# Second layer norm of six sequences: two ScalarE activations each in place of one VectorE operation

## The reference, cut to what matters

```python
x = x + tanh(g_xattn) * attention(layernorm(x), ctx, ctx, mask, Wq, Wk, Wv, Wo)   # 32 heads, 8 kv heads
x = x + tanh(g_ffn)   * ffn(layernorm(x), 4-bit gate, up and down weights)        # inner width 1376

def layernorm(x): return (x - mean(x)) / sqrt(var(x) + 1e-5)
```

## Time and profile before

| | us |
|---|---|
| median of 3 runs | 774.27 (773.15 to 774.89) |
| the profiled execution | 772.95 |
| its span, first to last instruction | 771.1 |
| granted TensorE clock, mean | 0.983 of full speed |
| `score(59)` to the first product of sequences 4 to 7 (start to start) | 540.70 to 605.39 |

### The profile page before, as it was taken

How to read it: one execution, slowest core, us unless ns; L and a number is a source line. 1 busy time by engine, 2 the same in 40 slices (tenths; PEclk the granted TensorE clock), 3 DMA queues, 4 the chain that set the end, 5 groups by cost and what they waited for, 6 DMA issues and landing times. The chain is left out here.

```text
span 771.1 us, 11053 instructions
## 1 busy us (share of the span) xinstructions
PE 727.8 (94%) x3394; PEld 602.3 (78%) x3394; DVE 602.1 (78%) x924; ACT 430.2 (56%) x777; POOL 509.8 (66%) x386
## 2 busy tenths in 40 slices
PE   3989999999999999999999999999669689999998
PEld 3868888888888888888888888888546578888786
DVE  6688798878879887987888788888877678778521
ACT  4686666665666666566666656565543345555420
POOL 5577778776677877667777766775796376656400
PEclk9999999999999999999999999999999899999999
DMA  9421012001201200120120002003220234432011
GB/s 278 102 80 42 1 42 96 14 1 40 85 1 41 96 15 1 31 93 1 42 95 15 1 28 96 1 0 84 48 65 0 66 89 96 116 97 41 1 69 41
DMA packets 70621, 41.53 MB, mean 54 GB/s; under 512 B 23242, under 2 KB 63050, under 8 KB 70570
## 3 DMA queue, kind: packets, MB, share of 16 engines
q1 hardware_dynamic: 70570, 40.90, 18.6%
HBM read 38.77 MB, written 2.11 MB: 53 GB/s over the span
## 5 line engine op out<-in xcount | busy, mean ns | idle before, releaser
L583 POOL TENSOR_TENSOR aT_lo<-attn,aT_hi 128x512 fp32r<-128x512 f32 x64 | 83.1, 1298 | 94.5 <-ACT aT_hi L802 94.5
L55 PE MATMUL ps_o<-wo_hi,aT_hi 128*128 128x512 f32 x256 | 102.2, 399 | 1.8 <-POOL acc L589 1.6
L55 PE MATMUL bank_q<-xT_hi,wq_hi 128*128 128x512 f32 x256 | 100.2, 391 | 2.4 <-DVE qT_lo L964 2.4
L57 PE MATMUL ps_o<-wo_hi,aT_lo 128*128 128x512 f32 x256 | 100.6, 393 | 0.0
L56 PE MATMUL ps_o<-wo_lo,aT_hi 128*128 128x512 f32 x256 | 100.4, 392 | 0.0
L683 ACT CAST qT_hi<-bank_q 128x512 fp32r<-128x512 f32 x64 | 37.6, 587 | 112.4 <-DVE bank_q L958 112.4
L57 PE MATMUL bank_q<-xT_hi,wq_lo 128*128 128x512 f32 x256 | 99.9, 390 | 0.0
L56 PE MATMUL bank_q<-xT_lo,wq_hi 128*128 128x512 f32 x256 | 99.9, 390 | 0.0
L511 POOL TENSOR_TENSOR q_sin<-q_sin,q_tab 128x512 f32<-128x512 f32 x64 | 83.3, 1301 | 19.0 <-ACT q_sin L676 17.2
L503 POOL TENSOR_TENSOR probs<-probs,keepT 128x512 f32<-128x512 f32 x64 | 83.0, 1297 | 9.4 <-ACT probs L812 9.3
L950 DVE TENSOR_TENSOR bank_q<-bank_q,q_tab 128x512 f32<-128x512 f32 x64 | 44.7, 699 | 35.0 <-ACT q_sin L676 34.9
(11 more groups left out here) (217 smaller groups left out, 2075.9 us busy)
## 6 DMA issues: line engine op xcount, KB each, us to landing
wq_raw<-in_Wq SPq DMA_DIRECT2D x32, 256.0 KB, 2.8
wo_raw<-in_Wo SPq DMA_DIRECT2D x8, 1024.0 KB, 5.2
packed<-in_gate_q SPq DMA_DIRECT2D x40, 64.0 KB, 2.3
packed<-in_up_q SPq DMA_DIRECT2D x40, 64.0 KB, 2.3
packed<-in_down_q SPq DMA_DIRECT2D x10, 256.0 KB, 3.2
acc<-in_x SPq DMA_DIRECT2D x8, 256.0 KB, 5.2
cT_raw<-in_ctx SPq DMA_DIRECT2D x8, 256.0 KB, 5.7
wk_raw<-in_Wk SPq DMA_DIRECT2D x8, 256.0 KB, 2.6
```

The source lines that it names most:

```text
L55: nc.tensor.matmul(out, w_hi, m_hi, start=first, stop=False)
L57: return nc.tensor.matmul(out, w_lo, m_hi, start=False, stop=last)
L583: nc.gpsimd.tensor_tensor(aT_lo[:], attn[:], aT_hi[:].bitcast(F32), ALU.subtract).then_inc(a_split, 1)
```

## The change

For sequences 0 to 5, DVE no longer runs `norm2_apply`. It makes minus the mean instead, one operation of one element on each partition, between the aggregate and the addition of epsilon. ACT runs two activations in slot 59 + b, behind `norm2_hi(b-1)` and ahead of `round_ffn` where that stands: `centre2` adds minus the mean, `scale2` multiplies by 1/std in place. Sequences 6 and 7 are left as they were.

```diff
+NORM2_ACT = 6
...
+                def centre2(b):
+
+                    act.wait_ge(mean2, b + 1)
+                    wait(act, prep2_T, b - 1)
+                    nc.scalar.activation(xn2t[:, b % 2, :], acc[:, b, :], ACT.Identity,
+                                         bias=minus_mean[:, b, :]).then_inc(x2_centred, 1)
+
+                def scale2(b):
+
+                    act.wait_ge(rstd2, b + 1)
+                    act.wait_ge(x2_centred, b + 1)
+                    nc.scalar.activation(xn2t[:, b % 2, :], xn2t[:, b % 2, :], ACT.Copy,
+                                         scale=rstd[:, b, :]).then_inc(xn2, 1)
...
                     if s >= TAIL + 4:
                         norm2_hi(s - TAIL - 4)
+                    if TAIL + 3 <= s < TAIL + 3 + NORM2_ACT:
+                        centre2(s - TAIL - 3)
+                        scale2(s - TAIL - 3)
                     if s == TAIL + 5:
...
                     dve.wait_ge(moments2, b + 1)
+                    if b < NORM2_ACT:
+                        nc.vector.tensor_scalar(minus_mean[:, b, :], moments[:, b, 0:1], -1.0, None, ALU.mult).then_inc(mean2, 1)
                     nc.vector.tensor_scalar(rstd[:, b, :], moments[:, b, 1:2], EPS, None, ALU.add).then_inc(var2, 1)
...
                     for kj in k_of(s - 1):
                         add_k(kj)
-                    if s >= TAIL + 4:
-                        norm2_apply(s - TAIL - 4)
                     if TAIL + 5 <= s < TAIL + 9:
                         norm2_lo(s - TAIL - 5)
```

More of the change, by code:

```diff
@@ L237, in flamingo_block @@
         stats2, moments2, var2, rstd2, xn2 = sem("stats2"), sem("moments2"), sem("var2"), sem("rstd2"), sem("xn2")
+        mean2, x2_centred = sem("mean2"), sem("x2_centred")
         prep2_T, prep2_hi, prep2_lo = sem("prep2_T"), sem("prep2_hi"), sem("prep2_lo")
```

## The result

The changed kernel takes 776.87 us at the median of 10 runs (776.11 to 778.15), the kernel before, beside it, 774.60 us (10 runs, 772.33 to 776.95): a ratio of 1.0029, 95% interval 1.0017 to 1.0041. It is slower by 2.3 us, with 1.3 and 3.2 us as the ends of the interval. The forecast was 776.1 us, slower by 1.8.

A forecast was written before the change was run, and what follows sets the result against it. The prediction took a ring of waits among POOL, DVE, PE and ACT, not one engine, to bound the stretch. Delays less shorter POOL operations summed to +1.8 us on the 774.27 us median: 776.1 us, range 773.5 to 778.5.

The forecast's parts named there:

- The ring and who bounds it: From 546 to 594 us, POOL, DVE, PE and ACT release each other in turn; DVE waits 5.3 us for POOL.
- The pair in slot 59: ACT's two activations stand straight ahead of `p_hi`, for which POOL waits, and hold ACT for 1.38 us.
- Slot 60 hidden: ACT's pair for sequence 1 costs nothing, as POOL wants `p_hi` later; addition of sequence 2 late by 1.19 us.
- slot 61 the second wait: ACT waits for POOL's `rstd` with `round_ffn` and `p_hi` queued behind: 0.6 us net, addition of sequence 3 late by 1.82.
- Slot 63 "just hidden": POOL's `p_lo` would end at 584.0, when `weigh(63)` starts anyway, so the pair adds nothing; `weigh(63)` late by 1.8 us.
- "Priced at nothing" for the removal: Taking six normalising operations (0.54 us at best, 1.24 median) off DVE gains DVE nothing, since it then waits for POOL.
- "The feed-forward layer moves as a whole": From slot 64 on, PE starts the products of sequences 4 to 7 1.8 us late and everything behind shifts equally.
- the bound for the clock: PE's lower granted clock after gaps: gaps move but no new long one arises, worth -0.3 to +0.5 us.
- the ring has give (B): Rival: idle waits and the shorter `add_share` make good the first 1.4 us; 0 to +0.6, about 774.6 us, chance 0.18.
- DVE was the bound (D): Rival: DVE sets the moments' start, so removal gives -3.1, about 771.2 us; chance 0.12 together with the port-lock rule.
- ACT bounds each slot (C): Rival: waits for `rstd` also decide in slots 60 and 63, 0.8 each; +3.4 to +4, about 777.9 us, chance 0.14.
- The price put on the port lock: Rule that DVE and POOL lock each other out: 3.2 us back over six slots, 772.9 us; shares a chance of 0.12.

The follow-up runs named there:

- e4: Kernel before, with DVE's normalising of sequences 0 to 5 cut to one column of 512 and nothing added on ACT: 774.37 us, ratio 1.0006.
- e5: Changed kernel with a third ACT activation of the same size behind the pair of slot 59: 777.39 us, one run.
- e6: Changed kernel with a third ACT activation behind the pairs of slots 60 and 62: 777.71 us, one run.
- e9: Changed kernel with the ACT pairs of sequences 0 to 4 moved into the next slot behind the share's scaling, sequence 5's left: 774.69 us, ratio 1.0003.
- e2: Kernel before, with the ACT pair for sequence 0 alone and sequences 1 to 5 still normalised on DVE: 776.93 us, ratio 1.0037.
- e8: Changed kernel, unchanged, run and traced a second time: 777.40 us, one run.
- e1: Kernel before, unchanged, run and traced a second time: 774.19 us, one run.
- e12: Changed kernel with pairs 0 to 4 later, plus 20 spare PE matmuls around the transposes of sequence 7: 773.07 us, ratio 0.9976 against the kernel before.
- e11: Changed kernel with pairs 0 to 4 later and two roundings of slot 59 ahead of the last query rounding: 775.06 us, ratio 1.0000.
- e7: Changed kernel with all six ACT pairs moved into the next slot, behind the share's scaling: 775.18 us, ratio 0.9997 against the kernel before.
- e10: Kernel before, with the two roundings POOL waits for in slot 60 put ahead of the last query rounding: 774.94 us, ratio 0.9986.
- e3: Kernel before, with ACT pairs for sequences 1 to 5 and sequence 0 still normalised on DVE: 774.65 us, ratio 1.0007.

## Why the prediction was right

Measured were 776.87 us where 776.1 was forecast. Of the 0.8 us between them, 0.33 come from the kernel before, which had 774.60 us in place of 774.27, and 0.47 from the change, +2.27 us in place of +1.8; its interval, 1.3 to 3.2 us, holds the forecast. In the tail the number was right for the reason given. That the whole came so near is in part luck, since the traces have 1.1 to 1.3 us more behind the tail, for which the forecast's sum had nothing.

**The ring and who bounds it: right.** The delay enters at POOL's `p_lo` of slot 60 and goes once around the ring; DVE's idle time there grew from 1.16 to 3.55 us (3.7 forecast). e4 gives DVE's work back and finds 0.65 us; e5 and e6 put the same work on ACT in three places and find it at its whole length in one and at nothing in the others. No table load stands between the pairs: every trace has two, at 0.7 us and ahead of Silu.

**The pair in slot 59: right, with one gap too small.** 1.45 us in place of 1.38: a dependent activation started 0.10 us after its predecessor's end and not 0.04, the gap read from DVE behind POOL. The shorter addition came as priced (1.27 us in place of 1.46), and the addition of sequence 1 is late by 1.28 (1.27).

**Slot 60 hidden, slot 61 the second wait: right.** Late by 1.12 and 1.90 at the two additions (1.19 and 1.82). e9, which moves the pairs behind the roundings, has no delay left at either (early by 0.27 and 0.54).

**Slot 63 "just hidden": not quite.** `weigh(63)` waits for POOL's `p_lo`, which ACT's pair holds up, and is late by 1.99 in place of 1.8: the pair is 0.07 longer than forecast, and POOL's `rstd` starts 0.06 later behind the mask than before. (The forecast's "about 1.2 us after the mask" does not fit the kernel before, where the mask ends at 580.81 and `rstd` at 581.33, 0.5 later; the 1.15 for `p_hi` does.) A tenth of a microsecond is made good behind.

**"Priced at nothing" for the removal: right for this change, thin for its neighbours.** In e2 the operation of sequence 4, left on DVE, costs 0.7 us once the ring is late by 1.4. The cover in the kernel before was that POOL happened to stand idle for that half microsecond.

**"The feed-forward layer moves as a whole": wrong in the traces.** This is the step that failed there, and with it the bound for the clock, -0.3 to +0.5. The stretch behind the tail was longer by 1.26 us in the first pair of traces and by 1.05 in the second (e8 against e1), with 13 slow matmuls in place of 7. So by the traces the change costs 2.9 to 3.1 us, over the 2.8 to which the forecast's own bounds add up (it wrote 3.0); one of its signs of being wrong, a tail late by 1.8 and an end that is not, is there. The medians say 2.3: beyond the tail's 1.88 that leaves 0.4, with -0.6 and +1.3 as ends, so how much of this an average execution has is open. Why the slow stretch is longer is not shown either: the idle time just ahead of it is 4.07 and 1.40 us in the traces with 7 and in those with 13 alike. e12 shows that it goes when that idle time is filled, e9 and e11 that other orders have the short one.

**The rivals.** That the ring has give (B) is out by e5, that DVE was the bound (D) by e4. That ACT bounds each slot (C) is out by e6 for slots 60 and 62; in slot 63 ACT's pair does hold POOL up, but it adds 0.19 us there and not 0.8. The price put on the port lock, 772.9 us, takes 3.2 off a forecast that had 0.76 of it off already; without that it is 773.6. Rule and trace also agree, in the end, on the Trainium skill's "Perfetto Trace Analysis", section "Optimizing Scalar/DVE Operations", which keeps such work on an unsaturated DVE; but e9 shows that the loss was not the slower form of the operation but the place where it stood.

## What to carry to other kernels

Before work is moved to a less busy engine, find in its queue the instruction that another engine is waiting for, and put the moved work behind it: the same twelve activations cost 1.9 us in the tail in one order and nothing in the other. A share of busy time does not tell this; the bracket behind the waiting instruction does. And where PE stands idle just ahead of a long dense stretch, count the slow matmuls at its start before and after an edit, in more than one execution: six of them were worth 1.2 us in a trace here, two thirds of what the edit cost in the tail.

## What the runs showed of the hardware

A gap on PE costs more than its own length. Behind the idle time of 4.1 and 1.4 us ahead of the first product of sequences 4 to 7, 6 to 13 matmuls ran spaced 0.43 us in place of 0.23, at a granted clock of 0.50, which is the lower of the two levels (1.2 in place of 2.4 GHz). The number was the same in both traced executions of a kernel (7 and 7, 13 and 13), but the times of e7 and e10 do not bear their 13 out. With 20 spare matmuls in the gap it was 0, at a granted clock of 1.00 over 25 us in place of 0.86 and 0.82, and the stretch behind was 2.6 us shorter than in e9. The same happened inside the tail: a projection of twelve matmuls ran at a granted clock of 0.50 from end to end in e3 and e10, and with it e10, early by 0.69 at the addition of sequence 2, was late by 0.81 at the next; e11, where it was not slow, was still early by 0.69 there.
